# Where the edge steps, the graph copies, the expert biases and the slot tables run in a fused graph, mixer and expert kernel

## The reference

```python
xn = _layernorm(x, axis=-1)
x = x + _L0_gnn_ref(xn, edge_attr_3, src, dst, ...) + _L0_mix_ref(xn[None], ...)[0]
x = x + _L0_ffn_ref(_layernorm(x, axis=-1)[None], ...)[0]

# graph layer
m = concatenate([h[edge_src], w]);  tmp = relu(m @ W1.T + b1)
h_N = segment_sum(tmp, edge_dst);   h_lin = relu(concatenate([h, h_N]) @ W2.T)
return h_lin / maximum(norm(h_lin), 1e-12)

# mixer, 4 layers
h = layernorm(x); x = x + linear_attention(h)   # softmax of q over features, of k over rows
h = layernorm(x); x = x + gelu(h @ W1 + b1) @ W2 + b2

# experts, 16 of them, the best 2 of each row
logits = x @ gate_w + gate_b; two largest, softmax over the two
h = relu(x @ w1[e] + b1[e]); y = x + sum_k weight_k * (h @ w2[e] + b2[e]); layernorm(y)
```

## Time and profile before

| | us |
|---|---|
| median of 3 runs | 2355.5 (2350.81 to 2363.58) |
| the profiled execution, its own time | 2356.42 |
| its span, first to last instruction | 2354.7 |

### The profile page before, as it was taken

The page is one execution under the profiler, slowest core; times in us unless marked ns, Lnnn a source line. Parts: engine busy times, 40 slices in busy tenths (PEclk is TensorE's granted clock), DMA queues, the critical chain, the costliest instruction groups (busy, mean ns, idle before and its releaser), DMA issues.

```text
span 2354.7 us, 33082 instructions
## 1 busy us (share of the span) xinstructions
PE 1992.1 (85%) x10654; PEld 1640.4 (70%) x10654; DVE 1524.8 (65%) x3442; ACT 925.8 (39%) x1947; POOL 1373.6 (58%) x1125
## 2 busy tenths in 40 slices
PE   2359899999888999988899998889999785799990
PEld 1337677777776778877677787767778574788880
DVE  4758867776787777678767777876766457411116
ACT  1224444443444444444444434454444231233330
POOL 4156566677556666756666675666667501566650
PEclk7769999999999999999999999999999885899995
DMA  8652222233322233333222233322223521799997
GB/s 212 183 148 72 69 71 71 73 78 101 87 72 70 72 74 75 85 104 76 67 73 73 71 84 105 89 72 73 70 72 84 118 77 44 236 305 303 302 280 169
DMA packets 269780, 268.49 MB, mean 114 GB/s; under 512 B 146075, under 2 KB 203486, under 8 KB 269630
## 3 DMA queue, kind: packets, MB, share of 16 engines
q0 software_dynamic: 127488, 134.76, 23.7%
q1 hardware_dynamic: 138030, 131.85, 19.1%
q10 hardware_dynamic: 4112, 0.03, 0.1%
HBM read 230.37 MB, written 35.05 MB: 113 GB/s over the span
## 4 chain that ended last, share of the span: by engine, by line
PE 58%; DVE 18%; DMA 10%; ACT 5%; issue 5%; POOL 2%; SPq 2%; DVEq 1%; POOLq 0%; ACTq 0%
PE bank L1205 21%; PE bank L1314 14%; PE bank L433 3%; DVE zl L455 3%; PE bank L434 3%; PE bank L441 3%; DMA xs<-zn_d,slot_tok 2%; PE bank L1215 2%; PE bank L1432 2%; DMA aT<-attr_d 2%; PE bank L1254 2%; PE bank L1440 2%; DVE z L481 2%; ACT zr L449 1%; DMA y_d<-yo,slot_row 1%
## 5 line engine op out<-in xcount | busy, mean ns | idle before, releaser
L843 POOL DMA_INDIRECT G<-P_d,src_T x896 | 1141.9, 1274 | 658.5 <-DVE z L481 388.6
L481 DVE TENSOR_TENSOR z<-bank,G 125x512 f32<-125x512 f32 x448 | 288.4, 685 | 174.4 <-PE bank L441 122.0
L1205 PE MATMUL bank<-W_s,hid 128*125 128x256 f32 x1600 | 366.6, 383 | 26.3 <-DVE qe L1616 26.3
L449 ACT ACTIVATE zr<-z 125x512 fp32r<-125x512 f32 x448 | 266.4, 629 | 304.8 <-DVE z L481 272.6
L455 DVE SCALAR_TENSOR_TENSOR zl<-z,zr 125x512 fp32r<-125x512 f32 x448 | 295.9, 702 | 130.4 <-ACT zr L449 125.9
L1314 PE MATMUL bank<-TT,W_s 128*128 128x250 f32 (+1 forms) x1280 | 352.9, 428 | 0.0
L1205 PEld LDWEIGHTS bank<-W_s,hid 128*125 128x125 f32 x1600 | 296.2, 190 | 73.5 <-issue 30.8
L1314 PEld LDWEIGHTS bank<-TT,W_s 128*128 128x128 f32 x1280 | 238.0, 191 | 93.9 <-issue 2.3
L433 PE MATMUL bank<-zr,onehot 125*125 125x256 f32 x896 | 268.2, 332 | 29.5 <-DVE zl L455 29.3
L1013 ACT ACTIVATE hid<-bank,b_s 128x375 f32<-128x375 f32 x320 | 166.6, 522 | 191.4 <-PE bank L1314 167.2
L434 PE MATMUL bank<-zl,onehot 125*125 125x256 f32 x896 | 227.0, 284 | 0.0
(11 more groups left out here) (313 smaller groups left out, 3019.6 us busy)
## 6 DMA issues: line engine op xcount, KB each, us to landing
W_s<-in_L_ffn_w SPq DMA_DIRECT2D x64, 512.0 KB
hid<-in_L_ffn_w SPq DMA_DIRECT2D x64, 512.0 KB
G<-P_d,src_T POOLq DMA_INDIRECT x896
W_s<-in_L_mix_W SPq DMA_DIRECT2D x8, 1024.0 KB, 10.5
aT<-attr_d SPq DMA_DIRECT2D x224, 31.2 KB
attr_d<-hn SPq DMA_DIRECT2D x12, 246.1 KB, 3.7
X<-in_x SPq DMA_DIRECT2D x5, 560.0 KB
P_d<-es SPq DMA_DIRECT2D x25, 112.0 KB
```

The lines of the kernel that those rows point to most:

```text
L449: nc.scalar.activation(zr[:, s, k, :], z[:, k, :], ACT.Relu).then_inc(r_done, 1)
L481: nc.vector.tensor_tensor(z[:, k, :], edge_bank[k][0:ET, :], G[:, ST * s + 2 * k:ST * s + 2 * k + 2, :].rearrange("p j d -> p (j d)"), ALU ...
L843: pool.indirect_dma_start(G[:, j, :], None, P_d[:, :], bass.IndirectOffsetOnAxis(ap=src_T[:, at:at + 1], axis=0)).then_inc(g_in[j], 16)
L1205: ins = pe.matmul(to[0:T, (j - a) * D:(j - a) * D + D], w, m, start=n == 0, stop=n == len(pairs) - 1)
```

## The change

- One more step is laid into the key phase of layers 0 and 2, in the second group. All 224 steps then lie within the mixer, and only the last step's sums follow it. The number of rounds is read early, ahead of layer 0 (on POOL ahead of its first gather).
- In the graph output, ACT's copies for `agg` of group g+1 and for the gate of g-1 stand ahead of the lengths of g (the gate's for g = 1 to 3).
- PE has both last gates ahead of all ranks.
- The experts of the slot tiles are found on DVE behind `ce`, with 64 partitions in place of one. SP starts the weights of the first two tiles from there, those of further tiles when the positions are known.
- The bias columns of all 64 tiles come from one table: 16 rows of `eb1` are loaded, and PE multiplies them with a one-hot of the tile's expert (L1428, L1432 of the new kernel). The first DMA of ACT and the 64 loads of `b1e` are gone.
- `inv_tile` is made by ACT (one operation of 3200 elements, and 25 of 64) and DVE (one product of 1600), and POOL has no part in it.

```diff
-        ST_K = [2, 2, 3, 2, 2]
+        ST_K = [[2, 3 - l % 2, 3, 2, 2] for l in range(L)]
...
-        def more_rounds(eng, tables, first, middle, last):
+        def round_count(eng):
             eng.wait_ge(rounds_done, 1)
-            rounds = eng.value_load(rounds_i[0:1, 0:1], min_val=1, max_val=ROUNDS)
+            return eng.value_load(rounds_i[0:1, 0:1], min_val=1, max_val=ROUNDS)
+
+        def more_rounds(eng, rounds, tables, first, middle, last):
             with eng.If(rounds > 1):
...
-            attr_steps(step_k(L, 0), NPAIR)
...
+            sp.wait_ge(edges_done, 1)
+            sp.dma_start(eb1_s, eb1).then_inc(b1_in, 16)
...
-                load(b1e[s][:, :], b1_all[:, ds(ex * NFE, NFE)], w1_in[s])
...
+            for m in range(MT):
+                if m == 2:
+                    sp.wait_ge(r_pos, 1)
+                expert_tile(m)
...
-            pool.wait_ge(r_split, 3)
-            for k in range(2):
-                pool.tensor_tensor(inv_tile[:, k, :, MT:2 * MT], chosen[:, k, :, :],
-                                   tok_t[:, :].unsqueeze(2).to_broadcast([T, NT, MT]), ALU.mult).then_inc(r_half, 1)
...
-                act.dma_start(b1_all[:, :].rearrange("p (h j) -> p h j", j=2), eb1.rearrange("e (h p j) -> p (e h) j", p=128, j=2)).then_inc(b1_in, 16)
...
             for g in range(NG):
                 if g + 1 < NG:
                     pairs_T(ring_x[g + 1], QT)
+                    pairs_T(ring_agg[g + 1], TT)
+                if 1 <= g < NG - 1:
+                    pairs_T(ring_z[g - 1], eT)
                 lengths(g)
-                if g + 1 < NG:
-                    pairs_T(ring_agg[g + 1], TT)
-                if g >= 1:
+                if g == NG - 1:
                     pairs_T(ring_z[g - 1], eT)
...
+            act.wait_ge(r_split, 3)
+            act.activation(inv_tile[:, :, :, 0:MT].rearrange("p k t m -> p (k t) m"), chosen[:, :, :, :].rearrange("p k t m -> p (k t) m"),
+                           ACT.Copy, scale=tok_p[:, :]).then_inc(r_half, 1)
+            for t in range(NT):
+                ins = act.activation(inv_tile[:, 1, t, MT:2 * MT], chosen[:, 1, t, :], ACT.Copy, scale=float(t + 1))
+            ins.then_inc(r_half, 1)
+            act.wait_ge(r_hot, 1)
+            act.activation(hotT[:, :], bank[2][0:NE, 0:MT], ACT.Copy).then_inc(r_hot, 1)
+            act.wait_ge(r_hot, 3)
+            act.activation(b1_t[:, :, :].rearrange("p c m -> p (c m)"), bank[2][:, 128:128 + NFE * MT], ACT.Copy).then_inc(r_hot, 1)
...
             gate(NG - 2)
-            for g in range(NG - 2):
+            gate(NG - 1)
+            for g in range(NG):
                 ranks(g)
-            gate(NG - 1)
-            ranks(NG - 2)
-            ranks(NG - 1)
...
             for k in range(2):
+                if k == 0:
+                    pe.wait_ge(ej_done, 2)
+                    pe.transpose(bank[2][0:NE, 0:MT], ej_hot[:, :], ident[0:MT, 0:MT]).then_inc(r_hot, 1)
+                    pe.wait_ge(r_hot, 2)
+                    pe.wait_ge(b1_in, 16)
+                    for c in range(NFE):
+                        ins = pe.matmul(bank[2][:, 128 + c * MT:128 + (c + 1) * MT], eb1_s[:, c // 2 * 256 + c % 2:c // 2 * 256 + 256:2], hotT[:, :],
+                                        start=True, stop=True)
+                    ins.then_inc(r_hot, 1)
                 pe.wait_ge(inv_cp, k + 2)
                 pe.wait_ge(r_half, k + 1)
```

More of the change, by code:

```diff
@@ L267, in build @@
             SC[:, 2 * KD * F + NFE * D * i:2 * KD * F + NFE * D * (i + 1)].rearrange("p (c d) -> p c d", d=D) for i in range(2)]
-        b1e = [sb(f"b1e{i}", [128, NFE]) for i in range(XB)]
         b2e = [brow[:, D * i:D * i + D] for i in range(XB)]
@@ L890, in _ @@
             act.sem_inc(xcopied, GT)
-            with nc.allow_non_contiguous_dma(reason="short vectors to columns"):
-                act.dma_start(b1_all[:, :].rearrange("p (h j) -> p h j", j=2), eb1.rearrange("e (h p j) -> p (e h) j", p=128, j=2)).then_inc(b1_in, 16)
             act.wait_ge(wT_T, 1)
@@ L938, in _ @@
                 both(e)
+            rounds = round_count(act)
             def step(ge):
@@ L1044, in _ @@
             pairs_T(ring_x[0], QT)
-            for e in range(EG_LAST, NEG):
-                both(e)
-            more_rounds(act, act_tables, lambda r: both(r * NEG), lambda e, ge: both(ge), lambda r: both(r * NEG + (NEG - 1)))
+            more_rounds(act, rounds, act_tables, lambda r: both(r * NEG), lambda e, ge: both(ge), lambda r: both(r * NEG + (NEG - 1)))
             def lengths(g):
@@ L1087, in expert_tile @@
                     slots_T(u, (s + 1) % 2)
-                hidden(u + (0 if last else 1), s)
+                hidden(u + (0 if last else 1), s, m)
             slots_T(RING_E, 0)
@@ L1772, in _ @@
                         keep_stats(g, l * NT + g * GT + NT, a_aggr, a_mv)
-            for e in range(EG_LAST, NEG):
-                both(e, e, last=e == NEG - 1)
             dve_acc(NPAIR - 1, block_of(NPAIR - 1))
@@ L1784, in tables @@
                 dve.wait_ge(t_cp, r * 5 + 5)
-            more_rounds(dve, tables, lambda r: both(0, r * NEG, first=True), lambda e, ge: both(e, ge), dve_last)
+            more_rounds(dve, rounds, tables, lambda r: both(0, r * NEG, first=True), lambda e, ge: both(e, ge), dve_last)
             dve.memset(counted[:, 0:NE], 0.0).then_inc(edges_done, 1)
@@ L1890, in _ @@
             dve.wait_ge(r_split, 2)
+            then(dve.tensor_scalar(ejf[:, :], ejf[:, :], float(-NE), None, ALU.add))
+            dve.tensor_scalar(ej_hot[:, :], iota_e[0:MT, :], ejf[:, :], None, ALU.is_equal).then_inc(ej_done, 1)
             dve.wait_ge(zn_out, NG * 32)
```

79 lines of the change are left out of this document (41 added, 38 removed).

## The result

| | before | after |
|---|---|---|
| median, us | 2355.5 | 2374.91 (2369.35 to 2386.76, 5 runs) |
| ratio | | 1.0077, 95% interval 1.0041 to 1.0114 |
| the profiled execution, us | 2356.42 | 2386.76 |

The changed kernel is slower by 19.4 us; 2348 was forecast, with 2333 to 2362 as the range. The profiled execution of after is the slowest of its five, 11.9 us above their median. Experiment 1 points at the experts, since it has the same expert code and a pace that is 0.26 us a tile better.

A forecast was written before the change was run, and what follows sets the result against it. It took the bound to differ by stage: PE with DVE and ACT chains, PE and DMA close together in the experts. Terms summed to -7.4 from the profiled 2356.4 us, 2349.0; against the median 2348, range 2333 to 2362.

The forecast's parts named there:

- No `b1e` loads: Experts: dropping the bias loads saves DMA time, -7 us, between 0 and -16.
- rival C: Experts: the bias loads were free, 0 in place of -7, so 2355 us; chance 0.13.
- Copies ahead of the lengths: Graph output: lengths start later, delaying DVE, with slow PE products behind longer gaps; +11 us, between +3 and +20.
- the clock at the start: Start of the graph output: a shorter PE gap may avoid the 1.2 GHz level; -1.2 us, between 0 and -2.4.
- Rival A: Graph output: the copies pay, PE sets the pace; -4 in place of +11, so 2333 us; chance 0.19.
- Rival B: Graph output: much slower, second and third pieces wholly at 1.2 GHz; +26 in place of +11, 2363 us; chance 0.11.
- No steps behind the mixer: Mixer's end: memset and `agg`'s transposes come earlier, -15.9 us; two steps laid within the mixer cost +5.2.
- The additions' hold on DVE: Mixer's end: POOL's earlier additions stall a `zl` pair that PE waits for; +2.4 us, between 0 and 6.
- Early load of the rounds: Ahead of layer 0: the load now stands in series on DVE, +0.6 us, hidden on POOL.
- ACT's first DMA: Kernel start: its removal frees DMA engines for rows and small biases; -1.5 us, between 0 and -2.9.
- Both gates ahead of the ranks: End of the graph output: DVE's wait for the last gate goes; -2.8 us.
- Router: Router: slot products end later, PE waiting for ACT's operations; +1.8 us, between -1 and +5.

The follow-up runs named there:

- Experiment 1: Changed kernel with ACT's lengths of each group again ahead of the copies for `agg` and the gate: 2363.4 us beside 2360.0 of before, 1.0018.
- experiment 4: Kernel before without the 64 bias loads and ACT's first DMA, relu taking 1.0 as bias: 2371.8 us beside 2360.0 of before, 1.0048.
- 2: Changed kernel with the 64 bias loads and ACT's first DMA put back, table still made: 2361.3 us beside 2360.0 of before, 1.0016.
- 8: Kernel before without the bias loads, POOL's gathers issued one tile earlier: 2349.2 us beside 2358.3 of before, 0.9964.
- 9: Kernel before with only POOL's gathers issued one tile earlier: 2336.4 us beside 2358.8 of before, 0.9911.
- experiment 5: Kernel before without the bias loads, the small `b2e` load moved between the two weight loads: 2358.1 us beside 2358.3 of before, 0.9998.
- 14: Kernel of 11 with input rows of groups 1, 2, 4 and normalised rows of group 2 behind the edges: 2331.1 us, 0.9889 of before.
- 11: Kernel of 10 with gathers one tile earlier and POOL's additions held until the edges are done: 2327.8 us beside 2358.3 of before, 0.9881.
- experiment 3: Kernel before with SP's loop over the weight loads written out: 2355.7 us beside 2360.0 of before, 0.9992.
- 10: Changed kernel with the old copy order, bias loads put back and table by products left out: 2348.2 us beside 2358.3 of before, 0.9965.

## Why the prediction was wrong, point by point

*No `b1e` loads, forecast -7.* This step failed, and with it the sign. Measured: about +12 (experiment 4; +14 for the changed kernel against 2, and +12 in 8 against 9, with early gathers). The prediction priced the packets as time on engines at their limit. But 303 GB/s were not the limit (9), and PE's waits for `xs` were the sign to read: POOL issued the gathers too late, and they take 5.3 to 5.9 us to land (medians of the nine traces that have the landing). What goes with the missing loads is a longer way for the two weight transfers: they land in 4.9 to 5.9 us, with the loads in 3.8 to 4.4. With the 1.5 KB transfer of experiment 5 they land in 4.8 to 5.0, and the whole loss is back. Why a small transfer between them helps stays open. The rival C (free) and the Trainium skill's rule for small pieces ("DMA: Bandwidth & Descriptors", "Why small descriptors are slow (HBM only)") would have given 2355 and were nearer, but wrong as well: nothing in either lets their removal cost 12 us. Another section of that page of the Trainium skill, "Queues, rings and completion order", says that each DMA engine takes turns between the queues that have work. That alone gives no reason why the order within SP's queue should matter to a gather on POOL's. In experiment 4 it did: PE waited 28.7 us for gathered rows, against 14.2 in 5, where the small load stands between.

*Copies ahead of the lengths, forecast +11, and -1.2 for the clock at the start.* Measured +13.0 from memset to last lengths for both together, +13.3 by experiment 1. The mechanism and its rows came out as told: 6.9 us for the delay, 8.5 us of idle PE, products at 1.2 GHz behind it. The size was 3 us short. Between the lengths of groups 0 and 1 it is 5.7 us, where the sum had 1.4 and its share of the 6 for the clock, and the -1.2 did not come: the first transposes still take 2.31 us and the first four products 1.91. The Trainium skill's rule on the clock ("TensorE: Matmul & The Clock Gate", Part 1) held for the gate, which went to full clock in four of five groups (2.33 us); the loss moved to the second piece, on which DVE's chain hangs. Rival A is refuted. Rival B lies the same way and would have been +26.

*No steps behind the mixer, -15.9 + 5.2 + 2.4.* Measured from the first `z` to the memset: -3.1 in the two profiles. Over the nine profiles with the steps inside it is 1732.3 us on average (1723 to 1737), over the eight others 1738.0 (1735 to 1742), so -5.7. But five of the nine hold POOL's additions back; the four that don't, like the changed kernel, have 1733.6, so -4.4 in place of -8.3. Two terms were mis-sized. The branch was taken at 2.9 us of idling and measured 6.2, with SP's row loads now just ahead of it (14). The additions' hold on DVE cost 4.6 (11), not 2.4. Timeline of PE in after, which answers to the earlier trace rows:

```profile
182.89 2.69 PE L1269 MATMUL bank<-TT,Wk_s 128*128 128x375 f32 x8
...
202.55 2.69 PE L1269 MATMUL bank<-TT,Wk_s 128*128 128x375 f32 x8
```

The second group, with its third step, takes 19.66 us. Before it took 17.41 (180.91 to 198.32): 2.25 for the step. In layer 2 it was 3.51 (22.75 against 19.24). 2.57 each was forecast.

*Early load of the rounds, ACT's first DMA, +0.6 and -1.5.* The first `z` begins at 128.3 to 131.8 us in all seventeen profiles, whatever they contain. These terms are below what can be seen.

*Both gates ahead of the ranks, -2.8.* Right: from the last lengths to the last `logits` 15.8 us in place of 18.5. The size is in part luck: in experiments 3 and 4, which have the old order, the last gate ran at full clock (2.32 and 2.45 us for 4.22), and there it is 16.6 and 16.7.

*Router, +1.8.* Measured -0.3. ACT's 3200 elements took 2.96 us (2.9 forecast), the 25 short operations 3.73 (5.4 forecast): 0.15 each, cheaper than the relus of 128 elements from PSUM by which they were sized. That PE waits for ACT was right. Without the table the slots come 3.2 us sooner (10), as its copy and products had stood on the way.

*Weights earlier, 0.* From `slot_tok` to the first scaled tile it is 20.0 us in both. Right.

Of the 27 us between forecast and result the bias loads are 19, the graph output 3, the edges and the branch 4, the router -2. The rest is less than the interval of the measurement.

The forecast and its rivals all had the bias loads between free and dear, none as a help. So the range ended at 2362. The rows named late gathers, not weights, as what PE waited for; what the loads did to the weight transfers beside them no row told.

## What to carry to other kernels

Here a DMA share near 1 and a rate of 303 GB/s did not mean that transfers were the limit: the named wait, for gathers that one queue issued too late, was, and moving their issue one tile ahead gave 22 us with one edit. When a transfer is dropped, ask what stood before and behind it on its queue, and not only what its bytes cost; and test a suspected middle step (here the late gathers) by taking it away in both kernels. And a copy or a wait that is moved off PE's path is no gain if the chain that PE waits for next starts later: price the longer gap with the slow clock behind it.

## What the runs showed of the hardware that was not expected

- Two 512 KB transfers issued back to back landed in 5.5 and 5.6 us, and PE waited 28.7 us for the gathers beside them; with a 1.5 KB transfer between them they landed in 5.0 and 4.8 us, and PE waited 14.2 us (1.0048 against 0.9998 of before). With 1.7 us between their issues and no transfer it was 1.0026.
- The branch, from the last addition to the memset, took 3.6 to 3.8 us where SP's row loads had been issued over 10 us ahead of it, 3.95 with one of 0.6 MB 2.1 us ahead, and 6.4 to 7.3 us where 1.3 to 2.6 MB of them were issued from 2.1 us ahead on.
- POOL's addition of 1280 elements held a DVE operation. Two of them in a row made a table of 0.67 us take 4.81, and in before a pair of 1.29 us take 7.47; three in a row made that pair take 10.29 (experiment 3).
- A PE wait of 2.54 us in the experts was followed by products at 1.2 GHz, and cost 1.6 us more than its own length.
